# Narrow attention: three of a pair's 52 exponentials computed on VectorE, their probabilities applied later

## The chip, the cores and the metric

One core of a Trainium2 chip runs the whole program. The metric is the device time of one execution in microseconds (us); the time before is the median of three runs. The profile comes from one further execution, recorded by the hardware profiler. Engines are named as in the profile: PE (TensorE matmuls), PEld (TensorE weight loads), DVE (VectorE), ACT (ScalarE), POOL (GpSimd), SP (SyncE).

## The reference, cut to what matters

The reference is a stack of gated cross-attention and feed-forward layers over 2048 tokens of width 256. The change touches one of them, the second cross-attention layer (its tiles are called `c_...` in the profile):

```
q = layernorm(x) @ Wq + bq     # 2048 queries, 16 heads of 16 columns
k = ctx @ Wk + bk              # 1601 keys
v = ctx @ Wv + bv
o = softmax(q k^T / 4) v       # per head
x = x + gate * (o @ Wo + bo)
```

Per head that is 2048 x 1601 exponentials. They are taken without a maximum first as long as a bound on the scores is small, and the sum is divided out at the end: a column of ones in the values gives the sum with the same matmuls.

## The kernel before, in words

The heads go in eight pairs. The keys of one head are 13 tiles (`CT`): twelve of 128 keys and one of 65. A pair therefore has 26 tiles (`TILES`), numbered 0 to 25, head 0 of the pair first. The 2048 queries are split in two halves of 1024, `hp` 0 and 1, so one pair has 52 steps, n = 2t + hp. Each step passes through three stages:

- **Score n** (TensorE, L1888): two matmuls, one on each half of the array's rows, write 128 keys x 1024 queries of scores to two PSUM banks. There are three such double banks, used in turn (`STEP_BANKS`), so score n may be written only when step n-3 has been read.
- **Exponential n** (ScalarE, L1969): one ACTIVATE of 128 x 1024 from PSUM to a buffer `probs` in SBUF. There are four such buffers, `2 * (t % 2) + hp` (they lie in the tiles `c_cT` and `c_wqkv`, whose names the profile shows). The exponential of tile t waits until tile t-2 has been applied, since that tile used the same buffer.
- **Apply t** (TensorE, L1908): four matmuls, one for each 512 queries, each on its own 32 columns of the array, in fp32 and so recorded as two passes each (eight records). They add the tile's values times its probabilities to bank 4 (head 0) or 5 (head 1). Apply t waits for exponential 2t+1.

TensorE runs them in one written order. For each tile t it is: score 2t+3, score 2t+4, apply t. The last two tiles of a pair are t = 24: score 51, score 0 of the next pair, apply 24; and t = 25: score 1 of the next pair, apply 25, then score 2 of the next pair. When a head is complete, VectorE copies the sums (L1987), TensorE turns them with four transposes (L1918: after tile 1 of the next pair for head 1, after tile 14 for head 0), and VectorE divides (L1990, L1994). VectorE also copies each head's values with their ones into `Vh` (L1981). That is all VectorE does here. SyncE loads the next pair's keys and queries when `applied` says that the old ones are free. TensorE's and ScalarE's programs are written out for all pairs; VectorE's pairs 1 to 7 are a loop at run time, so its waits count from a register. A second branch, with maxima, exists for scores above a bound.

Semaphores count the stages: `scored`, `exped`, `applied`, `copied`, `turned`, `normed`, `values_in`.

Of the kernel before, what the change touches and what calls it, by code (L numbers as in the profile page):

```python
# [17 lines left out]
int32 = mybir.dt.int32  # L18
ALU = mybir.AluOpType
# [3 lines left out]
P = 128  # L23
# [3 lines left out]
CT = -(-CTX // P)  # L27
# [3 lines left out]
BANK = 512  # L31
# [1388 lines left out]
CH_HEADS, CH_D = 16, 16  # L1420
GROUP = 4


LH, LD = 8, 64
INNER = LH * LD
# [101 lines left out]
def narrow_attention(nc, m, ci, rows_d, wo_d, bo_d, q_parts, k_parts, pw):  # L1527
# [5 lines left out]
    with ExitStack() as own:  # L1533
# [4 lines left out]
        with ExitStack() as inner:  # L1538
            si = lambda n, s, d=fp32: inner.enter_context(nc.sbuf_tensor(f"c_{n}", s, d))
# [282 lines left out]
            Vh = [si(f"Vh{i}", [P, CT, 32]) for i in range(2)]  # L1822
# [7 lines left out]

            STEP_BANKS = [(0, 2, 6)[n % 3] for n in range(2 * TILES - 1)] + [2]

            EXPED_FOR = {0: -3, 1: 0, 2: -1, 2 * TILES - 1: 2 * TILES - 2}
# [8 lines left out]
            with nc.Block() as block:  # L1842
                @block.sync
                def _(sp):

                    pw.load(sp, qkv_raw, 0)
                    for h in range(2, CH_HEADS):
                        sp.wait_ge(applied, (h - 1) * CT)
                        load_k(sp, h)
                        load_q(sp, h)  # L1850

# [5 lines left out]
                def _(pe):  # L1857
# [19 lines left out]
                    def score(i, n, first=False):  # L1877

                            t, hp = n // 2, n % 2
                            e, r, c0 = t // CT, krows(t), t % CT * P  # L1880
                            if t % CT == 0 and hp == 0:
                                pe.wait_ge(ops_in[e], (i + 1) * OPERANDS)
                            if n >= 3 or not first:
                                pe.wait_ge(exped, i * (2 * TILES) + EXPED_FOR.get(n, n - 2))
                            for b in range(2):
                                q0 = (2 * hp + b) * BANK
                                rows = slice(64 * b, 64 * b + 64)
                                last = nc.tensor.matmul(m.PS[0:r, STEP_BANKS[n] + b, :], Kop[e][rows, c0:c0 + r],  # L1888
                                                        Qop[e][rows, q0:q0 + BANK], start=True, stop=True)
                            last.then_inc(scored, 1)  # L1890

                    def take_maxima(i):

                        pe.wait_ge(row_cleared, i + 1)
                        pe.wait_ge(exped, i * (2 * TILES))
                        for e in range(2):
                            pe.wait_ge(ops_in[e], (i + 1) * OPERANDS)
                            maxima(e, (i * 2 + e) * MAX_REDUCED)
                        pe.wait_ge(max_reduced, (i + 1) * (2 * MAX_REDUCED))

                    def pair(i, first=False, last_pair=False, guarded=False):
                        def apply(t):
# [3 lines left out]
                            pe.wait_ge(exped, i * (2 * TILES) + (2 * t + 2))  # L1906
                            for q in range(4):
                                last = nc.tensor.matmul(m.PS[32 * q:32 * q + 32, 4 + e, :], Vh[e][0:r, t % CT, :],  # L1908
                                                        probs[2 * (t % 2) + q // 2][0:r, (q % 2) * BANK:(q % 2 + 1) * BANK],
                                                        start=(t % CT == 0), stop=(t % CT == CT - 1),  # L1910
                                                        tile_position=(0, 32 * q))
                            last.then_inc(applied, 1)

                        def turn(e, n):

                            pe.wait_ge(copied, n + 1)
                            for j in range(4):
                                last = nc.tensor.transpose(m.PS[:, 4 + e, j * P:(j + 1) * P], outT[e][:, j * P:(j + 1) * P],  # L1918
                                                           m.ident[:])
                            last.then_inc(turned, 1)  # L1920

                        for t in range(TILES):
                            for n in range(2 * t + 3, min(2 * t + 5, 2 * TILES)):
                                score(i, n)

                            if not last_pair and not guarded and t >= TILES - 2:
                                score(i + 1, t - (TILES - 2))
                            apply(t)
                            if t == TURN_AT and not first:
                                turn(1, i * 2 - 1)  # L1930
                            if t == CT + 1:
                                turn(0, i * 2)
                        if not last_pair and not guarded:
                            score(i + 1, 2)
                        if not last_pair and guarded:
# [23 lines left out]
                @block.scalar  # L1959
                def _(act):  # L1960
                    nc.scalar.preload_act_table(ACT.Exp)
                    for i in range(CH_HEADS // 2):
                        for n in range(2 * TILES):
                            t, hp = n // 2, n % 2
                            act.wait_ge(scored, i * (2 * TILES) + (n + 1))
                            if i * TILES + t > 1:
                                act.wait_ge(applied, i * TILES + t - 1)
                            r = krows(t)
                            nc.scalar.activation(probs[2 * (t % 2) + hp][0:r, :],  # L1969
                                                 m.PS[0:r, STEP_BANKS[n]:STEP_BANKS[n] + 2, :].rearrange(  # L1970
                                                     "p b c -> p (b c)"), ACT.Exp).then_inc(exped, 1)

                @block.vector
                def _(dve):
                    bits = dve.value_load(bound[0:1, 0:1].bitcast(int32))

                    def pair(i, first=False):
# [6 lines left out]
                        def output(e, n):  # L1984

                            dve.wait_ge(applied, n * CT + CT)
                            nc.vector.tensor_copy(outT[e][:], m.PS[:, 4 + e, :]).then_inc(copied, 1)  # L1987
                            dve.wait_ge(turned, n + 1)
                            out = m.PS[:, 4 + e, :].rearrange("p (j q d) -> p j q d", q=4, d=32)
                            nc.vector.reciprocal(inverse[e][:], out[:, :, :, CH_D]).then_inc(inverted, 1)  # L1990
                            dve.wait_ge(inverted, n + 1)

                            dst = attended[:, :, ds(n * CH_D, CH_D)].rearrange("p (q j) d -> p j q d", q=4)
                            nc.vector.tensor_tensor(dst, out[:, :, :, 0:CH_D],  # L1994
                                                    inverse[e][:].unsqueeze(3).to_broadcast([P, 4, 4, CH_D]),
                                                    ALU.mult).then_inc(normed, 1)

                        with dve.If(bits > SAFE_BITS):
                            dve.wait_ge(rows_in, 128)
                            dve.wait_ge(exped, i * (2 * TILES))  # L2000
                            for e in range(2):
                                for row in MAX_ROWS:
                                    last = nc.vector.memset(Qop[e][row:row + 1, :], 0.0)
                            last.then_inc(row_cleared, 1)
                            for e in range(2):
                                score_maxima_dve(nc, m, dve, spans, partial, negated, MAX_ROWS,
                                                 [Qop[e][row:row + 1, :] for row in MAX_ROWS], max_scored, max_reduced,
                                                 (i * 2 + e) * MAX_SCORED, (i * 2 + e) * MAX_REDUCED)
                        place_values(0)
                        if not first:  # L2010
                            output(1, i * 2 - 1)
# [7 lines left out]
                    output(1, CH_HEADS - 1)  # L2019

        add_projected(nc, m, "c_out", attended, wo, bo[:].rearrange("p t d -> p (t d)"), m.gate[:, 1:2])

# [1042 lines left out]
```

## Time and profile before

| | us |
|---|---|
| Median of three runs (3122.47 to 3125.54) | 3123.19 |
| The profiled execution's own time | 3124.35 |
| Its span | 3122.6 |
| The narrow attention's stretch of it, first score to last apply | 1960 to 2346 |

The profile's first part gives busy time by engine over the whole span; its second part cuts the span into 40 slices of 78 us, and the narrow attention fills slices 26 to 30 and a part of the next. A time in a timeline is counted from the start of the span. In an x8 row of L1908 the eight pass records of one apply are merged, so its duration is that of the whole apply. An ACTIVATE's start is when it enters its engine, which can be before the one ahead of it has ended; the distance from end to end is what one costs when they follow each other.

### The profile page before, as it was taken

Reading aid. Unit: us, or ns where it says so; the run is one execution under the profiler, and the core shown is the slowest. Engines: PE = TensorE matmul, PEld = TensorE weight load, DVE = VectorE, ACT = ScalarE, POOL = GpSimd, SP = SyncE. Lnnn points to the kernel's source line nnn. Section 1 sums busy time; section 2 is a strip of 40 time slices with the busy share of each in tenths; the row PEclk is TensorE's granted clock in tenths of the full one; section 3 lists DMA queues with packets and bytes.
Section 4 is the critical chain, followed back from the end, with each engine's and each line's share of the span. In section 5 each row is a group of like instructions: output and inputs, shape, how many; then the busy total and the mean of one; then the engine's idle time right before and its main releaser. Section 6 shows DMA issues by size and latency. Waiting matters only on the chain. (4 is left out here: it accounts for less than half of the span.)

```text
span 3122.6 us, 71606 instructions
## 1 busy us (share of the span) xinstructions
PE 2913.0 (93%) x29570; PEld 1454.7 (47%) x29570; DVE 2233.9 (72%) x2810; ACT 1944.9 (62%) x2644; POOL 518.9 (17%) x573
## 2 busy tenths in 40 slices
PE   5999999999999999999999899999996997989979
PEld 3444444444444444444444455222224766556755
DVE  6888888888889888888878875100006886768866
ACT  5665655656656656656556524899993775247642
POOL 0000000000001000000000010200002773247710
PEclk8999999999999999999999989999998999999999
DMA  2000000000000000000000011111101000000000
GB/s 81 9 2 7 3 2 7 3 2 9 2 7 4 2 7 3 2 2 3 2 2 2 28 38 63 56 28 36 29 19 53 15 8 25 36 14 18 5 1 28
DMA packets 30102, 51.69 MB, mean 17 GB/s; under 512 B 6136, under 2 KB 22603, under 8 KB 28619
## 3 DMA queue, kind: packets, MB, share of 16 engines
q1 hardware_dynamic: 29770, 46.91, 4.8%
q8 instruction: 253, 4.15, 0.6%
q14 instruction: 79, 0.64, 0.1%
HBM read 41.04 MB, written 5.83 MB: 15 GB/s over the span
## 5 line engine op out<-in xcount | busy, mean ns | idle before, releaser
L771 ACT ACTIVATE a_probs<-PS 128x1024 f32<-128x1024 f32 x928 | 950.0, 1025 | 572.2 <-PE PS L524 561.4
L537 PE MATMUL PS<-a_probs,a_V 64*64 64x512 f32 x7424 | 984.2, 590 | 6.7 <-DVE a_heads_outT L958 5.0
L1018 DVE TENSOR_TENSOR a_prob_sums<-a_prob_sums,a_probs 128x1024 f32<-128x1024 f32 x512 | 628.5, 1228 | 111.6 <-ACT a_probs L771 85.9
L1015 DVE SCALAR_TENSOR_TENSOR a_prob_sums<-a_probs,a_valid,a_prob_sums 128x1024 f32<-128x1024 f32 x384 | 508.6, 1325 | 73.1 <-ACT a_probs L771 59.4
L524 PE MATMUL PS<-a_Q_hi,a_K_hi 64*64 64x512 f16 x3712 | 390.4, 381 | 6.0 <-ACT a_probs L771 4.9
L524 PE MATMUL PS<-a_Q_hi,a_K_lo 64*64 64x512 f16 x3712 | 387.1, 377 | 2.2 <-issue 2.2
L524 PE MATMUL PS<-a_Q_lo,a_K_hi 64*64 64x512 f16 x3712 | 386.9, 377 | 0.0
L537 PEld LDWEIGHTS PS<-a_probs,a_V 64*64 64x64 f32 x7424 | 293.4, 133 | 168.1 <-issue 23.0
L1969 ACT ACTIVATE c_cT<-PS 128x1024 f32<-128x1024 f32 (+1 forms) x312 | 303.3, 1082 | 1.6 <-PE PS L1908 0.8
L67 POOL CAST a_heads_hi<-a_heads_outT 128x512 f16<-128x512 f32 x31 | 49.6, 1601 | 1444.8 <-DVE a_heads_outT L974 1444.8
L524 PEld LDWEIGHTS PS<-a_Q_hi,a_K_hi 64*64 64x64 f16 x3712 | 119.8, 106 | 260.3 <-issue 254.2
L524 PEld LDWEIGHTS PS<-a_Q_hi,a_K_lo 64*64 64x64 f16 x3712 | 120.6, 107 | 226.2 <-issue 222.0
L1987 DVE COPY c_outT<-PS 128x512 f32<-128x512 f32 x16 | 11.1, 692 | 296.4 <-PE PS L1908 296.4
L1908 PE MATMUL PS<-c_cT,c_Vh 128*32 128x512 f32 (+1 forms) x1248 | 221.1, 607 | 0.3 <-ACT c_wqkv L1969 0.3
L2275 ACT ACTIVATE d_probs<-d_scores,d_minus_max 128x256 f32<-128x256 f32 x256 | 127.0, 497 | 120.3 <-DVE d_minus_max L2440 120.3
L1888 PE MATMUL PS<-c_Qop,c_Kop 64*128 64x512 f16 (+1 forms) x832 | 154.6, 388 | 28.6 <-ACT c_cT L1969 6.7
L524 PEld LDWEIGHTS PS<-a_Q_lo,a_K_hi 64*64 64x64 f16 x3712 | 121.0, 107 | 88.7 <-issue 1.2
L1888 PEld LDWEIGHTS PS<-c_Qop,c_Kop 64*128 64x128 f16 (+1 forms) x832 | 38.6, 94 | 243.9 <-ACT c_cT L1969 194.5
L1969 ACT ACTIVATE c_wqkv<-PS 128x1024 f32<-128x1024 f32 (+1 forms) x104 | 112.9, 1085 | 0.0
L1908 PE MATMUL PS<-c_wqkv,c_Vh 128*32 128x512 f32 (+1 forms) x416 | 109.4, 605 | 0.0
L2543 POOL TENSOR_TENSOR d_crossed<-d_unit,d_tables 128x256 f32<-128x256 f32 x128 | 104.0, 842 | 6.1 <-DVE d_unit L2409 6.1
L2201 PE MATMUL PS<-ident,d_probs 128*128 128x128 f32 x512 | 69.0, 293 | 29.7 <-ACT d_kT L2290 29.7
(356 smaller groups left out, 4616.9 us busy)
## 6 DMA issues: line engine op xcount, KB each, us to landing
c_Qop<-q_part SPq DMA_DIRECT2D x96, 64.0 KB, 2.2
c_Kop<-k_part SPq DMA_DIRECT2D x96, 50.0 KB, 2.0
d_raw<-in_l1f_w_dram SPq DMA_DIRECT2D x18, 256.0 KB, 3.2
d_tables<-in_rotary_dram SPq DMA_DIRECT2D x2, 2048.0 KB, 11.4
X<-in_x_dram SPq DMA_DIRECT2D x2, 1024.0 KB, 9.4
out_dram<-X SPq DMA_DIRECT2D x8, 256.0 KB, 2.2
c_cT<-in_ctxT_dram SPq DMA_DIRECT2D x1, 1601.0 KB, 6.4
a_probs<-in_ctx_dram SPq DMA_DIRECT2D x3, 512.0 KB, 4.9
```

The costliest lines, as they stand in the source:

```text
L67: return engine.tensor_copy(hi, x)
L524: last = nc.tensor.matmul(m.PS[64 * g:64 * g + 64, 2 * (n % 2) + h, :], k[rows, half_keys], q[rows, queries], start=(j == 0), stop=(j == l ...
L537: last = nc.tensor.matmul(m.PS[64 * h:64 * h + 64, PVB + g, :], V[e][rows, s, 64 * h:64 * h + 64], probs[n % 4][rows, h * BANK:(h + 1) * B ...
L771: nc.scalar.activation(probs[n % 4][:], m.PS[:, b0:b0 + 2, :].rearrange("p b c -> p (b c)"), ACT.Exp).then_inc(exped, 1)
L1015: nc.vector.scalar_tensor_tensor(out=sums, in0=new, scalar=valid[:, s:s + 1], in1=sums, op0=ALU.mult, op1=ALU.add).then_inc(summed, 1)
L1018: nc.vector.tensor_tensor(sums, sums, new, ALU.add).then_inc(summed, 1)
L1888: last = nc.tensor.matmul(m.PS[0:r, STEP_BANKS[n] + b, :], Kop[e][rows, c0:c0 + r], Qop[e][rows, q0:q0 + BANK], start=True, stop=True)
L1908: last = nc.tensor.matmul(m.PS[32 * q:32 * q + 32, 4 + e, :], Vh[e][0:r, t % CT, :], probs[2 * (t % 2) + q // 2][0:r, (q % 2) * BANK:(q % ...
L1969: nc.scalar.activation(probs[2 * (t % 2) + hp][0:r, :], m.PS[0:r, STEP_BANKS[n]:STEP_BANKS[n] + 2, :].rearrange("p b c -> p (b c)"), ACT.E ...
L2201: last = nc.tensor.transpose(m.PS[:, SCORE_BANK + 2 * g + p // 2, at:at + P], probs[:, 4 * g + p, kt * P:(kt + 1) * P], m.ident[:])
L2275: last = nc.scalar.activation(probs[:, p, :], scores[:, p, :], ACT.Exp, bias=minus_max[:, p:p + 1], accum_out=sums[:, p:p + 1])
L2543: last = nc.gpsimd.tensor_tensor(crossed[:, qk, :, a, :], unit[w % 2][:, qk, :, 1 - a, :], tables[:, 1, w, qk, a * 32:a * 32 + 32].unsquee ...
```

## The change

Three of a pair's 52 steps are taken by VectorE: both halves of tile 5 (steps 10 and 11) and the first half of tile 20 (step 40). ScalarE skips them. VectorE reads the scores from PSUM, scaled to powers of two and held above -126, in one instruction per step, which frees the bank (`taken`). It then rounds them with a large constant, subtracts, builds the power of two as an integer, and multiplies by a polynomial of degree five: eight further SBUF instructions (after the one or two that take the scores) and one that ends the batch. Steps 10 and 11 are one batch of 2048 columns, step 40 a batch of 1024. The result goes to a buffer of its own, `dve_probs`.

The applies of these steps move. Apply 5 comes behind apply 15. At tile 20 only the half that ScalarE made is applied; the other half is applied behind apply 25, ahead of score 2 of the next pair. The turn of head 0 moves from tile 14 to tile 17. `applied` now counts 27 events per pair in place of 26, and the waits on it and on `exped` are rewritten to match. The wait of an exponential on the reader of its buffer stays the reader two tiles back, save where that was a VectorE step: then it is four tiles back. The banks and their order are unchanged. On VectorE the order within a pair is: values of head 0, output of the last pair's head 1, values of head 1, batch of steps 10 and 11, output of head 0, batch of step 40.

```diff
+            BANK_FROM = {0: 2 * TILES - 4, 1: 2 * TILES - 1, 2: 2 * TILES - 2, 2 * TILES - 1: 2 * TILES - 3}
+            DVE_TILE, DVE_HALF = 5, (CT + 7, 0)
+            DVE_STEPS = (2 * DVE_TILE, 2 * DVE_TILE + 1, 2 * DVE_HALF[0] + DVE_HALF[1])
+            TILE_AT, HALF_AT, TURN_FIRST_AT = CT + 2, TILES - 1, CT + 4
...
-                                pe.wait_ge(exped, i * (2 * TILES) + EXPED_FOR.get(n, n - 2))
+                                owner = BANK_FROM.get(n, n - 3)
+                                back = 1 if n < 3 else 0
+                                if owner in DVE_STEPS:
+                                    pe.wait_ge(taken, i * N_DVE + (DVE_STEPS.index(owner) + 1 - back * N_DVE))
+                                else:
+                                    pe.wait_ge(exped, i * N_ACT + (acted_to(owner) + 1 - back * N_ACT))
...
-                            apply(t)
+                            if t != DVE_TILE:
+                                apply(t, tuple(hp for hp in range(2) if (t, hp) != DVE_HALF))
+                            if t == TILE_AT:
+                                apply(DVE_TILE, (0, 1))
+                            if t == HALF_AT:
+                                apply(DVE_HALF[0], (DVE_HALF[1],))
                             if t == TURN_AT and not first:
                                 turn(1, i * 2 - 1)
-                            if t == CT + 1:
+                            if t == TURN_FIRST_AT:
                                 turn(0, i * 2)
...
                         for n in range(2 * TILES):
+                            if n in DVE_STEPS:
+                                continue
                             t, hp = n // 2, n % 2
                             act.wait_ge(scored, i * (2 * TILES) + (n + 1))
-                            if i * TILES + t > 1:
-                                act.wait_ge(applied, i * TILES + t - 1)
+                            reader = t - 2
+                            if 2 * reader + hp in DVE_STEPS:
+                                reader -= 2
+                            if i * TILES + reader >= 0:
+                                back = 1 if reader < 0 else 0
+                                act.wait_ge(applied, (i - back) * N_EVENTS + event_of(reader + back * TILES, hp))
...
+                        def exponentials(steps, at):
+                            w = len(steps) * 2 * BANK
+                            x, whole, out = exp_in[:, 0:w], exp_whole[:, 0:w], dve_probs[:, 0:w]
+                            count = i * (2 * EXP_STEPS) + at * EXP_STEPS
+                            for k, n in enumerate(steps):
+                                dve.wait_ge(scored, i * (2 * TILES) + (n + 1))
+                                nc.vector.tensor_scalar(exp_in[:, k * 2 * BANK:(k + 1) * 2 * BANK],
+                                                        m.PS[:, STEP_BANKS[n]:STEP_BANKS[n] + 2, :].rearrange("p b c -> p (b c)"),
+                                                        EXP_LOG2E, EXP_LEAST, ALU.mult, ALU.max).then_inc(taken, 1)
+                            dve.wait_ge(taken, i * N_DVE + (DVE_STEPS.index(steps[-1]) + 1))
+                            nc.vector.tensor_scalar(whole, x, EXP_MAGIC, -EXP_MAGIC, ALU.add, ALU.add).then_inc(exp_step, 1)
+                            dve.wait_ge(exp_step, count + 1)
+                            nc.vector.tensor_tensor(x, x, whole, ALU.subtract).then_inc(exp_step, 1)
+                            dve.wait_ge(exp_step, count + 2)
+                            nc.vector.tensor_scalar(whole.bitcast(int32), whole, 127.0, float(2 ** 23), ALU.add,
+                                                    ALU.mult).then_inc(exp_step, 1)
+                            nc.vector.tensor_scalar(out, x, EXP_TERMS[5], None, ALU.mult).then_inc(exp_step, 1)
+                            for j, k in enumerate((4, 3, 2, 1)):
+                                dve.wait_ge(exp_step, count + (4 + j))
+                                nc.vector.scalar_tensor_tensor(out=out, in0=out, scalar=EXP_TERMS[k], in1=x, op0=ALU.add,
+                                                               op1=ALU.mult).then_inc(exp_step, 1)
+                            dve.wait_ge(exp_step, count + EXP_STEPS)
+                            nc.vector.scalar_tensor_tensor(out=out, in0=out, scalar=EXP_TERMS[0], in1=whole, op0=ALU.add,
+                                                           op1=ALU.mult).then_inc(dve_exped, 1)
...
-                        output(0, i * 2)
+                        exponentials(DVE_STEPS[0:2], 0)
+                        output(0, i * 2, i * N_EVENTS + HEAD_END[0])
+                        exponentials(DVE_STEPS[2:3], 1)
```

## Rows read from the trace of the kernel before

**Rows 1.** The page: span and busy time by engine; granted clock in 40 slices.
```profile
span 3122.6 us, 71606 instructions
PE 2913.0 (93%) x29570; PEld 1454.7 (47%) x29570; DVE 2233.9 (72%) x2810; ACT 1944.9 (62%) x2644; POOL 518.9 (17%) x573
PEclk8999999999999999999999989999998999999999
```

**Rows 2.** Stretches of narrow attention: from:to length, busy of each engine, granted clock, DMA.
```profile
2104.00:2152.00 48.00, 44.77 (x324) 9.74 (x320) 3.92 (x8) 47.90 (x53) 0.00 (x0) 1.00 0.12 30
1960.00:2346.00 386.00, 358.48 (x2556) 77.59 (x2556) 29.89 (x61) 383.33 (x417) 18.86 (x18) 1.00 0.11 31
```

**Rows 3.** Timeline of ACT: start us, us, engine, line, operation, tiles.
```profile
2041.87 1.02 ACT L1969 ACTIVATE c_wqkv<-PS 128x1024 f32<-128x1024 f32 x1
...
2052.72 1.17 ACT L1969 ACTIVATE c_wqkv<-PS 128x1024 f32<-128x1024 f32 x1
```

**Rows 4.** Who waited for whom, 2008 to 2344: engine, line, us, times, longest.
```profile
DVE c_outT L1987 <- PE PS L1908: 251.9, 14, 18.2
PEld PS L1888 <- ACT c_cT L1969: 169.7, 238, 1.3
```

**Rows 5.** Timelines of ACT, then PE, one tile amid a head.
```profile
2121.04 2.03 ACT L1969 ACTIVATE c_cT<-PS 128x1024 f32<-128x1024 f32 x2
2122.85 1.14 ACT L1969 ACTIVATE c_wqkv<-PS 128x1024 f32<-128x1024 f32 x1
...
2122.21 0.39 PE L1888 MATMUL PS<-c_Qop,c_Kop 64*128 64x512 f16 x2
2122.53 1.06 PE L1908 MATMUL PS<-c_cT,c_Vh 128*32 128x512 f32 x8
2123.53 0.91 PE L1888 MATMUL PS<-c_Qop,c_Kop 64*128 64x512 f16 x4
```

**Rows 6.** Timeline of PE where one pair passes into the next.
```profile
2104.24 1.06 PE L1908 MATMUL PS<-c_cT,c_Vh 128*32 128x512 f32 x8
2105.42 0.39 PE L1888 MATMUL PS<-c_Qop,c_Kop 64*128 64x512 f16 x2
2105.74 0.62 PE L1908 MATMUL PS<-c_cT,c_Vh 65*32 65x512 f32 x2
...
2106.21 0.60 PE L1908 MATMUL PS<-c_wqkv,c_Vh 65*32 65x512 f32 x2
2106.74 1.07 PE L1888 MATMUL PS<-c_Qop,c_Kop 64*128 64x512 f16 x6
2107.74 1.06 PE L1908 MATMUL PS<-c_cT,c_Vh 128*32 128x512 f32 x8
```

**Rows 7.** Timeline of ACT at the same place; its exponentials 0 and 1.
```profile
2105.43 1.94 ACT L1969 ACTIVATE c_cT<-PS 128x1024 f32<-128x1024 f32 x2
```

**Rows 8.** Groups of DVE by form: busy us, mean ns of one | idle before.
```profile
L2432 DVE TENSOR_TENSOR d_scores<-PS,d_masks 128x1024 f32<-128x1024 f32 x64 | 77.7, 1213 | 3.4 <-PE PS L2133 2.5 <-PE PS L2138 0.9
L1011 DVE TENSOR_SCALAR a_prob_sums<-a_probs,a_valid 128x1024 f32<-128x1024 f32 x32 | 24.1, 753 | 39.4 <-ACT a_probs L771 39.4
L1018 DVE TENSOR_TENSOR a_prob_sums<-a_prob_sums,a_probs 128x1024 f32<-128x1024 f32 x512 | 628.5, 1228 | 111.6 <-ACT a_probs L771 85.9 <-DVE a_prob_sums L1018 0.9 <-DVE a_prob_sums L1015 0.5
L1015 DVE SCALAR_TENSOR_TENSOR a_prob_sums<-a_probs,a_valid,a_prob_sums 128x1024 f32<-128x1024 f32 x384 | 508.6, 1325 | 73.1 <-ACT a_probs L771 59.4
L67 DVE CAST b_W_hi<-b_W1T 128x2048 f16<-128x2048 f32 x1 | 1.2, 1226 | 0.0
```

**Rows 9.** Timeline of DVE in a chain of dependent instructions on small tiles.
```profile
2986.91 0.15 DVE L2709 SCALAR_TENSOR_TENSOR d_work<-d_work 128x4 f32<-128x4 f32 x1
2987.11 0.16 DVE L2711 TENSOR_TENSOR d_work<-d_work 128x4 f32<-128x4 f32 x1
```

**Rows 10.** Timeline of PE: the turn of head 1, and the scores behind it.
```profile
2110.57 0.66 PE L1918 MATMUL PS<-ident,c_outT 128*128 128x128 f32 x4
2111.16 0.60 PE L1888 MATMUL PS<-c_Qop,c_Kop 64*128 64x512 f16 x4
```

More of the change, by code:

```diff
@@ L1421 @@
 GROUP = 4
+EXP_LOG2E, EXP_MAGIC, EXP_LEAST = float(np.log2(np.e)), 12582912.0, -126.0
+EXP_TERMS = (1.00000007, 0.69314697, 0.2402212, 0.05550713, 0.00967554, 0.00132765)
 LH, LD = 8, 64
@@ L1831, in narrow_attention @@
             STEP_BANKS = [(0, 2, 6)[n % 3] for n in range(2 * TILES - 1)] + [2]
-            EXPED_FOR = {0: -3, 1: 0, 2: -1, 2 * TILES - 1: 2 * TILES - 2}
+            BANK_FROM = {0: 2 * TILES - 4, 1: 2 * TILES - 1, 2: 2 * TILES - 2, 2 * TILES - 1: 2 * TILES - 3}
+            DVE_TILE, DVE_HALF = 5, (CT + 7, 0)
+            DVE_STEPS = (2 * DVE_TILE, 2 * DVE_TILE + 1, 2 * DVE_HALF[0] + DVE_HALF[1])
+            TILE_AT, HALF_AT, TURN_FIRST_AT = CT + 2, TILES - 1, CT + 4
+            N_DVE, N_ACT = len(DVE_STEPS), 2 * TILES - len(DVE_STEPS)
+            acted_to = lambda n: n - sum(d < n for d in DVE_STEPS)
+            EVENTS = []
+            for t in range(TILES):
+                if t != DVE_TILE:
+                    EVENTS.append((t, tuple(hp for hp in range(2) if (t, hp) != DVE_HALF)))
+                if t == TILE_AT:
+                    EVENTS.append((DVE_TILE, (0, 1)))
+                if t == HALF_AT:
+                    EVENTS.append((DVE_HALF[0], (DVE_HALF[1],)))
+            N_EVENTS = len(EVENTS)
+            event_of = lambda t, hp: next(i + 1 for i, (u, hps) in enumerate(EVENTS) if u == t and hp in hps)
+            HEAD_END = [max(event_of(t, hp) for t in range(e * CT, (e + 1) * CT) for hp in range(2)) for e in range(2)]
+            exp_in, exp_whole, dve_probs = (si(f"exp_{n}", [P, 4 * BANK]) for n in ("in", "whole", "probs"))
+            EXP_STEPS = 8
+            taken, dve_exped, exp_step = (m.sem(f"c_{n}") for n in ("taken", "dve_exped", "exp_step"))
             partial, negated = si("partial", [P, 1, 2, ST]), si("negated", [P, ST])
@@ L1847, in _ @@
                     for h in range(2, CH_HEADS):
-                        sp.wait_ge(applied, (h - 1) * CT)
+                        sp.wait_ge(applied, (h // 2 - 1) * N_EVENTS + (event_of(CT - 1, 0) if h % 2 == 0 else N_EVENTS))
                         load_k(sp, h)
@@ L1894, in take_maxima @@
                         pe.wait_ge(row_cleared, i + 1)
-                        pe.wait_ge(exped, i * (2 * TILES))
+                        pe.wait_ge(exped, i * N_ACT)
                         for e in range(2):
@@ L1901, in pair, with apply @@
                     def pair(i, first=False, last_pair=False, guarded=False):
-                        def apply(t):
+                        def apply(t, hps):
                             e, r = t // CT, krows(t)
@@ L1905, in apply @@
                                 pe.wait_ge(values_in, i * 2 + (e + 1))
[L1906 to L1910, printed above, removed]
+                            for hp in hps:
+                                if 2 * t + hp in DVE_STEPS:
+                                    pe.wait_ge(dve_exped, i * 2 + (1 if t == DVE_TILE else 2))
+                                else:
+                                    pe.wait_ge(exped, i * N_ACT + (acted_to(2 * t + hp) + 1))
+                            for q in range(2 * hps[0], 2 * hps[-1] + 2):
+                                if 2 * t + q // 2 in DVE_STEPS:
+                                    at = q if t == DVE_TILE else q % 2
+                                    p = dve_probs[0:r, at * BANK:(at + 1) * BANK]
+                                else:
+                                    p = probs[2 * (t % 2) + q // 2][0:r, (q % 2) * BANK:(q % 2 + 1) * BANK]
+                                last = nc.tensor.matmul(m.PS[32 * q:32 * q + 32, 4 + e, :], Vh[e][0:r, t % CT, :], p,
+                                                        start=(t % CT == 0),
+                                                        stop=(event_of(t, q // 2) == max(
+                                                            event_of(u, q // 2) for u in range(e * CT, (e + 1) * CT))),
                                                         tile_position=(0, 32 * q))
@@ L1927, in pair @@
                                 score(i + 1, t - (TILES - 2))
-                            apply(t)
+                            if t != DVE_TILE:
+                                apply(t, tuple(hp for hp in range(2) if (t, hp) != DVE_HALF))
+                            if t == TILE_AT:
+                                apply(DVE_TILE, (0, 1))
+                            if t == HALF_AT:
+                                apply(DVE_HALF[0], (DVE_HALF[1],))
                             if t == TURN_AT and not first:
                                 turn(1, i * 2 - 1)
-                            if t == CT + 1:
+                            if t == TURN_FIRST_AT:
                                 turn(0, i * 2)
@@ L1982, in place_values @@
                                                   ).then_inc(values_in, 1)
-                        def output(e, n):
-                            dve.wait_ge(applied, n * CT + CT)
+                        def exponentials(steps, at):
[22 more added lines that the diff above has]
+                                                           op1=ALU.mult).then_inc(dve_exped, 1)
@@ L1987, in output @@
+                        def output(e, n, end):
+                            dve.wait_ge(applied, end)
                             nc.vector.tensor_copy(outT[e][:], m.PS[:, 4 + e, :]).then_inc(copied, 1)
@@ L1999, in pair @@
                             dve.wait_ge(rows_in, 128)
-                            dve.wait_ge(exped, i * (2 * TILES))
+                            dve.wait_ge(exped, i * N_ACT)
                             for e in range(2):
@@ L2010, in pair @@
                         if not first:
-                            output(1, i * 2 - 1)
+                            output(1, i * 2 - 1, i * N_EVENTS)
                         place_values(1)
-                        output(0, i * 2)
+                        exponentials(DVE_STEPS[0:2], 0)
+                        output(0, i * 2, i * N_EVENTS + HEAD_END[0])
+                        exponentials(DVE_STEPS[2:3], 1)
                         return output
@@ L2018, in _ @@
                         output = pair(j + 1)
-                    output(1, CH_HEADS - 1)
+                    output(1, CH_HEADS - 1, CH_HEADS // 2 * N_EVENTS)
         add_projected(nc, m, "c_out", attended, wo, bo[:].rearrange("p t d -> p (t d)"), m.gate[:, 1:2])
```

## The prediction

> **What bounds the kernel now.** First the page: TensorE is busy 93% of the span and its clock is granted in full nearly everywhere [rows 1]. That average says nothing of this stage, so the second view is the stretches: in 48.00 us amid the narrow attention ScalarE is busy 47.90, TensorE 44.77, VectorE 3.92, at clock 1.00 [rows 2]. The reader should distrust the 44.77: it counts latency. The third view is ScalarE's timeline. Its exponentials end at 2042.89 and 2053.89, twelve apart, so one costs 0.917 us, end to end [rows 3]; 52 of them make 47.7 us (the two of 65 rows a little less), and a pair takes about 48. ScalarE is the bound, and the waits agree: score loads wait 169.7 us for ScalarE, VectorE's output 251.9 us for TensorE [rows 4], while ScalarE waits for nobody.
>
> But by how much is it the bound? That decides this change, and the timeline of one tile tells it [rows 5]. Write E, S, A for exponential, score and apply. An E ends at 2123.07, so the one before it at 2122.16, and S(2t+4) starts at 2122.21: 0.05. The apply starts 0.32 behind it (2122.53), lasts 1.06, and the next score starts at 2123.53, 1.00 after the apply did. A tile thus costs TensorE 1.00 + 0.32 + one more score. Two scores back to back last 0.60 [rows 10] against 0.39 for one [rows 5], so one slot is 0.21 to 0.23; TensorE needs 1.55 of the tile's 1.83 us. It has 0.28 to spare in a tile, and no more.
>
> There is a closed loop beside it. E(2t+4) writes the buffer that A t reads, and A t waits for E(2t+1). From the end of E(2t+1): 0.05 to the score, 0.32 to the apply, 1.06 for it, 0.13 to the start of E(2t+4) (an apply ends at 2105.30, the exponential starts at 2105.43 [rows 6, 7]), and 1.02 for it, as the unhurried ones last [rows 3, 7]: 2.59 us (the rounded terms make 2.58). Three exponentials take 2.75. **So the loop of four probability buffers stands only 0.16 us behind ScalarE.**
>
> **Part by part.** I set the end of the last pair's E51 to zero and follow one pair.
>
> *Removed:* three exponentials a pair, 3 x 0.917 = 2.75 us, in eight pairs 22.0 us of ScalarE. What of it comes back is what the loops let through.
>
> *Steps 10 and 11.* E12 is in tile 6 and waits for A4; A4 waits for E9. With 10 and 11 gone, E12 is the very next one, and it still ends 2.59 after E9. Before, it ended 2.75 after. Two exponentials removed return 0.16 us. ScalarE sits idle about 1.5 us in their place. The banks aren't late: E12 needs S12, E13 needs S13, which waits behind A4 anyway and for `taken`, done by then (below). Sum -0.16.
>
> *Apply 5 behind apply 15, and the turn at tile 17.* Let U be the end of E31. A15 starts U+0.37, A5 0.91 later (two passes of 0.455: in an apply the passes start at 2105.74 and 2106.2 [rows 6]), S35 at U+2.28, done +2.67, so E35 starts U+2.80 and ends +3.82, against 4 x 0.917 = 3.67. A16 then starts U+2.83, is done +3.89, and E36 ends U+5.04. A17 and the turn (0.59, from 2110.57 to 2111.16 [rows 10]) keep TensorE busy: S41 starts only at U+7.50, so E41 ends at U+9.04; S42 U+7.84, A19 U+8.16, done +9.22, E42 ends U+10.37. Before, E42 ended eleven exponentials behind E31, 10.08, plus 0.13 that the turn cost it (a delay of the same kind follows each turn). So this stretch, with step 40 taken out of it, comes to +0.16 us. The third removed exponential too returns nothing.
>
> *The second half of tile 20 behind apply 25.* This is new work: a half apply takes two of the array's four column groups for as long as a whole one, since the four matmuls of a pass run side by side (eight records of 0.60 in 1.06 us [rows 6]). Before, A25 started at 2105.74 and score 2 of the next pair at 2106.74 [rows 6]. It was done at 2107.13, and E2 followed E1 (end 2107.37 [rows 7]) without loss, ending 2108.28. Now score 2 starts at 2107.65, E2 starts at 2107.65 + 0.39 + 0.13 = 2108.17 and ends 2109.19: +0.90. In the last pair there is no next one, but the output waits 0.91 for it. TensorE could absorb it elsewhere (0.28 a tile); here two exponentials only are in store behind it.
>
> Per pair -0.16 + 0.16 + 0.90 = +0.90. It falls on seven passages, and the end adds 0.91: 7 x 0.90 + 0.91 = 7.2 us.
>
> *Terms that no row shows.* An apply behind an apply costs 0.91, if it follows as a pass follows a pass, or 1.00, as a score follows an apply. With 1.00 both late applies cost more, the pair +1.06: 8.5 in all. I lean to 0.91, the same form of instruction. Each apply now has two waits in place of one. Nothing in the trace shows a second wait on TensorE; it is 0 where it hides in the 0.32 between score and apply, and I bound it at 0.03 an apply, which in the tight places (about eight per pair) makes up to 1.6 us in all. Below: if a half apply costs half, 0.46, the passages cost 0.45 and the whole 3.6. I take 7.8 and keep 3.6 to 10.
>
> *VectorE, the cover of all this.* Reading 1024 scores from PSUM: 1.21 (L2432, the nearest row with PSUM) [rows 8]. In SBUF a one-input instruction of 1024 costs 0.75, of 2048 1.23 to 1.29 (the cast of 2048; 0.75 + 512 elements at the two-a-cycle slope), a two-input one 1.23 and 2.30, a scalar-tensor-tensor 1.33 and 2.40 [rows 8]; a dependent one follows after 0.05 (2987.06 to 2987.11) [rows 9]. First batch: 2 x 1.21 + 3 x 1.29 + 2.30 + 5 x 2.40 + 10 x 0.04 = 21.0. Second: 1.21 + 3 x 0.75 + 1.23 + 5 x 1.33 + 0.4 = 11.7. With the 3.92 of before, 36.6 of 48.8 us. What matters is lateness. E7 ends at 8.40 (1.09 for E0, seven pitches, and the 0.90 above), S10 follows at 8.45 and is done at 8.85, so the first batch ends at 30.0; A5 wants it at 31.5: 1.5 to spare. S40 is done at 36.8; VectorE has by then given out head 0 (its turn ends at 36.3), takes it at 37.2 and ends at 48.9; the half apply wants it at 50.05: 1.2 to spare. Values for the next pair (0.59) are wanted at 51.8. Step 11's bank is free at 11.5, score 14 wants it at 12.0; step 40's at 38.4, S43 wants it at 39.4. So VectorE costs nothing, with 1.2 us of margin. The bound above: all three one-input instructions at one element a cycle (2.30 and 1.23, as the two-input rows). That adds 3.0 to the first batch, 1.5 over its margin, and with it about 1.6 us per pair: +13.
>
> A page of the Trainium skill prices ScalarE itself. "VectorE: DVE Perf Modes", in its section on the TRN2 errata, gives PSUM to SBUF as 172 cycles plus one per element at 1.2 GHz, that is 0.997 us for 1024, an estimate by that page; the rows have 0.917 from end to end and 1.02 alone. By the page's price 24 exponentials would be 23.9 us rather than 22.0, and the loop would look slower than ScalarE by less; the rows decide. The same page's tier table gives fp32 `tensor_scalar` in SBUF two elements a cycle and anything from PSUM one, which rows 8 bear out for forms without a bitcast.
>
> **Sum.** 3124.35 + 7.8 = 3132.2 for a profiled run. The median before lies 1.16 below that run's own time, so 3131.0.
>
> **The rivals.**
> *It pays: ScalarE's time comes back.* If E12 and E42 really start behind E9 and E41, every pair gives back 2.75, pays 0.90 at its end and 0.3 at apply 5: -1.5 x 8, near 3111; half of it back gives 3120. For it: ScalarE busy 47.90 of 48.00. Against it: E0 starting 0.13 behind an apply's end [rows 6, 7], with its 1.02 alone, shows that the buffer wait is real, and each number of the loop is read off. It decides if the loop is under 1.8 us rather than 2.59. Chance 0.09.
> *Too small to tell* (0.2% is 6.2 us, about what a measurement of this kernel can tell from no change): the half apply at half its price, or one of the stalls milder than drawn: 3125 to 3129. Against the half price: the passes of four matmuls end together. The page "TensorE: Matmul & The Clock Gate", part 3 on packing, has tiles side by side for about 4 ns each, which is the same side; the sum doesn't use it. Chance 0.23, and in it is that the change does nothing at all.
> *VectorE is late.* 2.30 instead of 1.29, or 0.2 us between dependent steps: 3132 to 3145, with 3144 where all go at one element a cycle. For it: its waits count from registers in a loop, and no row has a bitcast. Against: margins of 1.2 and 1.5. Chance 0.18.
> *My forecast*, the ring closes and the half apply is paid: 3130 to 3134, chance 0.50.
>
> **How the numbers follow.** The likeliest case gives 3131.0. The range takes in the bounds of the small terms below (3126) and most of a late VectorE above (3145). Faster by over 0.2%: 0.09. Within: 0.23. Slower: 0.68.
>
> **What would show it.** ScalarE's timeline: a gap of about 1.5 us between E9 and E12 in every pair, released by L1908 and not by scores; a gap of 0.9 at E2 behind the passage, released by a score; end to end still 0.917 elsewhere; ScalarE busy near 45 of 48. Pairs 48.8 apart rather than 47.9. VectorE busy near 37 a pair, one-input instructions of 2048 near 1.3 us, and TensorE not waiting for its last instruction (the end of a batch). If pairs are 46 to 47 apart, the loop was wrong; if TensorE waits for VectorE before apply 5 or at the pair's end, the third rival is it.

## The result, and the profile after

The changed kernel takes 3129.9 us (median of 14 runs, 3126.71 to 3132.07) against 3123.53 for the kernel before in the same runs (14, 3118.55 to 3127.59). The ratio is 1.0021, with a 95% interval of 1.0013 to 1.0029: slower, by 6.4 us between the medians, and by more than noise. I had forecast 3131.0, which is 7.8 us above the median of the three runs before. The profiled execution took 3130.8 us, its span 3129.0.

The page of the changed kernel, against [rows 1]: ScalarE lost 19 us of busy time, VectorE gained 243, and the span is 6.4 us longer.

```profile
span 3129.0 us, 72043 instructions
PE 2915.5 (93%) x29570; PEld 1457.0 (47%) x29570; DVE 2477.1 (79%) x2978; ACT 1925.7 (62%) x2620; POOL 532.6 (17%) x573
```

In the changed kernel's own lines the exponentials are L2019, the scores L1917, the applies L1946. A stretch of 48 us amid the narrow attention, against [rows 2] (length, busy of PE, PEld, DVE, ACT, POOL, clock, DMA):

```profile
2110.00:2158.00 48.00, 44.06 (x318) 9.66 (x312) 33.72 (x29) 44.88 (x50) 0.00 (x0) 1.00 0.12 30
```

ScalarE now idles 3.1 of 48 us, so the relief arrived at the engine. It was not used. Who waited for whom between 2012 and 2348, against [rows 4], where ScalarE had no row:

```profile
ACT c_cT L2019 <- PE PS L1946: 15.9, 21, 1.6
...
ACT c_cT L2019 <- PE PS L1917: 4.8, 7, 0.7
PEld PS L1917 <- DVE c_exp_in L2041: 5.9, 7, 0.8
```

ScalarE waits for applies (L1946) 21 times, three times in each of the seven pairs of the window, and once a pair for a score (L1917). The waits for VectorE are only for the reads of its scores; no row has TensorE waiting for the end of a batch. The ScalarE timeline shows where, with the end of the last pair's E51 at 2106.67 (against [rows 7] and [rows 3]):

```profile
2105.61 1.06 ACT L2019 ACTIVATE c_wqkv<-PS 65x1024 f32<-65x1024 f32 x1
2106.70 1.94 ACT L2019 ACTIVATE c_cT<-PS 128x1024 f32<-128x1024 f32 x2
2109.32 1.02 ACT L2019 ACTIVATE c_cT<-PS 128x1024 f32<-128x1024 f32 x1 [0.69 <-PE PS L1917]
...
2114.95 1.94 ACT L2019 ACTIVATE c_cT<-PS 128x1024 f32<-128x1024 f32 x2
2118.46 2.85 ACT L2019 ACTIVATE c_cT<-PS 128x1024 f32<-128x1024 f32 x3 [1.57 <-PE PS L1946]
...
2140.79 2.86 ACT L2019 ACTIVATE c_cT<-PS 128x1024 f32<-128x1024 f32 x3 [0.27 <-PE PS L1946]
...
2146.13 1.02 ACT L2019 ACTIVATE c_cT<-PS 128x1024 f32<-128x1024 f32 x1 [0.42 <-PE PS L1946]
```

E2 waits 0.69 us for its score; E12 waits 1.57 for apply 4; E36 waits 0.27 and E42 waits 0.42 for applies. From the end of E9 (2114.95 + 1.94 = 2116.89) to that of E12 (start 2118.46, 1.02 long, 2119.48) are 2.59 us.

TensorE at the same two places: first the passage with the half apply, whose four records read `c_exp_probs`, against [rows 6]; then score 12, which follows the end of E9, and apply 4, against [rows 5].

```profile
2106.73 0.39 PE L1917 MATMUL PS<-c_Qop,c_Kop 64*128 64x512 f16 x2 [0.16 <-ACT c_wqkv L2019]
2107.05 0.62 PE L1946 MATMUL PS<-c_cT,c_Vh 65*32 65x512 f32 x2
...
2107.93 1.03 PE L1946 MATMUL PS<-c_exp_probs,c_Vh 128*32 128x512 f32 x4
2108.89 0.82 PE L1917 MATMUL PS<-c_Qop,c_Kop 64*128 64x512 f16 x6
...
2116.94 0.39 PE L1917 MATMUL PS<-c_Qop,c_Kop 64*128 64x512 f16 x2 [0.25 <-ACT c_cT L2019]
2117.26 1.07 PE L1946 MATMUL PS<-c_cT,c_Vh 128*32 128x512 f32 x8
```

VectorE's two batches in the same pair, against [rows 8]:

```profile
2115.42 2.54 DVE L2041 TENSOR_SCALAR c_exp_in<-PS 128x1024 f32<-128x1024 f32 x2 [0.52 <-PE PS L1917]
2117.99 1.23 DVE L2045 TENSOR_SCALAR c_exp_whole<-c_exp_in 128x2048 f32<-128x2048 f32 x1
2119.26 2.29 DVE L2047 TENSOR_TENSOR c_exp_in<-c_exp_in,c_exp_whole 128x2048 f32<-128x2048 f32 x1
2121.58 1.23 DVE L2049 TENSOR_SCALAR c_exp_whole<-c_exp_whole 128x2048 int32<-128x2048 f32 x1
...
2133.28 2.29 DVE L2057 SCALAR_TENSOR_TENSOR c_exp_probs<-c_exp_probs,c_exp_whole 128x2048 f32<-128x2048 f32 x1
...
2153.17 1.23 DVE L2057 SCALAR_TENSOR_TENSOR c_exp_probs<-c_exp_probs,c_exp_whole 128x1024 f32<-128x1024 f32 x1
```

The first batch runs from 2115.42 to 2135.57, the second ends at 2154.40. Apply 5 starts at 2138.09 and the half apply at 2156.6, which is 49.9 us after the end of the last pair's E51: 2.5 and 2.2 us of room for VectorE. The integer step with its bitcast (L2049) takes 1.23 us, as its one-input neighbour L2045 does.

Below, a pair's length is the distance from the end of the last pair's E51 to the end of its own (the first pair's is taken from the start of its E0). It was 47.91 us in every pair but the first, and is 48.66 to 48.67 now.

### The profile page after: what moved, and what is told of

The parts are those of the page before. It is cut to its first block and busy times, and to the rows that moved or that the text cites. A ratio compares the mean times of both kernels' runs of the same rounds, so it can differ in the third digit from the quotient of the medians.

```text
span 3129.0 us, 72043 instructions
## 1 busy us (share of the span) xinstructions
PE 2915.5 (93%) x29570; PEld 1457.0 (47%) x29570; DVE 2477.1 (79%) x2978; ACT 1925.7 (62%) x2620; POOL 532.6 (17%) x573
## 5 line engine op out<-in xcount | busy, mean ns | idle before, releaser
L771 ACT ACTIVATE a_probs<-PS 128x1024 f32<-128x1024 f32 x928 | 949.2, 1024 | 571.6 <-PE PS L524 567.0
L2019 ACT ACTIVATE c_cT<-PS 128x1024 f32<-128x1024 f32 (+1 forms) x296 | 286.5, 1055 | 25.1 <-PE PS L1946 19.0
L1946 PE MATMUL PS<-c_cT,c_Vh 128*32 128x512 f32 (+1 forms) x1184 | 212.6, 608 | 0.5 <-ACT c_wqkv L2019 0.5
L1917 PE MATMUL PS<-c_Qop,c_Kop 64*128 64x512 f16 (+1 forms) x832 | 149.1, 387 | 34.1 <-ACT c_cT L2019 16.3
L1917 PEld LDWEIGHTS PS<-c_Qop,c_Kop 64*128 64x128 f16 (+1 forms) x832 | 36.6, 94 | 235.8 <-ACT c_cT L2019 169.7
L2054 DVE SCALAR_TENSOR_TENSOR c_exp_probs<-c_exp_probs,c_exp_in 128x2048 f32<-128x2048 f32 (+1 forms) x64 | 113.7, 1776 | 2.2
L2019 ACT ACTIVATE c_wqkv<-PS 128x1024 f32<-128x1024 f32 x96 | 101.6, 1058 | 0.0
L1946 PE MATMUL PS<-c_wqkv,c_Vh 128*32 128x512 f32 (+1 forms) x384 | 101.0, 605 | 0.0
```

The costliest lines, as they stand in the source:

```text
L771: nc.scalar.activation(probs[n % 4][:], m.PS[:, b0:b0 + 2, :].rearrange("p b c -> p (b c)"), ACT.Exp).then_inc(exped, 1)
L2019: nc.scalar.activation(probs[2 * (t % 2) + hp][0:r, :], m.PS[0:r, STEP_BANKS[n]:STEP_BANKS[n] + 2, :].rearrange("p b c -> p (b c)"), ACT.E ...
L2054: nc.vector.scalar_tensor_tensor(out=out, in0=out, scalar=EXP_TERMS[k], in1=x, op0=ALU.add, op1=ALU.mult).then_inc(exp_step, 1)
```

## The experiments

All are compared with the kernel before, on the same chip.

**Tile 5 alone on VectorE** (`e1_tile_only`).

```diff
-            DVE_TILE, DVE_HALF = 5, (CT + 7, 0)
-            DVE_STEPS = (2 * DVE_TILE, 2 * DVE_TILE + 1, 2 * DVE_HALF[0] + DVE_HALF[1])
+            DVE_TILE, DVE_HALF = 5, None
+            DVE_STEPS = (2 * DVE_TILE, 2 * DVE_TILE + 1)
...
-                        exponentials(DVE_STEPS[2:3], 1)
```

> Only steps 10 and 11 go to VectorE (apply 5 behind apply 15, turn at tile 17); step 40 stays on ScalarE, so nothing is applied behind apply 25. Theory (the loop of four probability buffers): E12 still ends 2.59 us after E9, two exponentials removed return 0.16, and the late apply with the later turn takes 0.2 to 0.3 back: a pair lasts 48.0 us (47.9 before), the whole +0.9 us over before (0 to +2). E2 follows E1 without a gap. Rival, ScalarE's time comes back: pairs of 46.1 to 46.5, -11 to -15 us. Rival, VectorE's presence itself costs (PSUM port, memory): +5 us as the full change has.

Measured 3124.17 against 3122.53, ratio 1.0004 (0.9995 to 1.0013); pairs of 48.03 us. Two exponentials are gone and ScalarE still waits 1.57 us behind E9:

```profile
2114.27 1.94 ACT L2019 ACTIVATE c_cT<-PS 128x1024 f32<-128x1024 f32 x2
2117.77 2.86 ACT L2019 ACTIVATE c_cT<-PS 128x1024 f32<-128x1024 f32 x3 [1.57 <-PE PS L1946]
```

This part of the change, with two thirds of its relief, gives nothing back and costs 0.12 us a pair: E12 comes 0.16 earlier, and the late apply 5 with the later turn takes 0.28 again. VectorE's work isn't what costs either: its batch is 20 us a pair here.

**The half of tile 20 alone** (`e2_half_only`).

```diff
-            DVE_TILE, DVE_HALF = 5, (CT + 7, 0)
-            DVE_STEPS = (2 * DVE_TILE, 2 * DVE_TILE + 1, 2 * DVE_HALF[0] + DVE_HALF[1])
+            DVE_TILE, DVE_HALF = None, (CT + 7, 0)
+            DVE_STEPS = (2 * DVE_HALF[0] + DVE_HALF[1],)
...
-                        exponentials(DVE_STEPS[0:2], 0)
```

> Only step 40 goes to VectorE, its half applied behind apply 25. Theory: the cost of the change is this half apply. E2 of the next pair is 0.76 late as in the full change, step 40 returns 0.16 to 0.2 and the turn at tile 17 a little: pairs of 48.35 (47.9 before), the whole +3.9 us over before (+3 to +5). Rival, the cost lies in apply 5 and batch one: 0 to +1 us. Rival, ScalarE's time comes back: pairs of 47.0, -7 us.

Measured 3126.3, ratio 1.0012 (1.0003 to 1.0022), +3.8 us by the medians; pairs of 48.42. E2 ends 3.67 us after the last E51, as with the full change (3.68), against 2.92 before.

**The full change without the half apply** (`e5_no_half_apply`).

```diff
-                if t == HALF_AT:
-                    EVENTS.append((DVE_HALF[0], (DVE_HALF[1],)))
...
-                            if t == HALF_AT:
-                                apply(DVE_HALF[0], (DVE_HALF[1],))
```

> The full change, but the half apply behind apply 25 is left out (VectorE still makes its probabilities, and they are used by nobody: the output lacks one half tile's share). Theory: of the change's 0.75 us a pair all is this apply, by way of score 2; without it E2 follows E1, and pairs last 47.8 (47.9 before, 48.66 with the change), the whole -1 to +1 us against before. Rival: the cost is VectorE's work or ScalarE's idle time: pairs stay near 48.5, +5 us.

Measured 3123.26 against 3122.62, ratio 1.0003 (0.9994 to 1.0012); pairs of 47.87, where the change has 48.66. Together with e2 this settles where the cost lies: the 0.75 us a pair that the change costs is the half apply at the passage. (This kernel leaves one half tile's share out of the output.) What is left of the change, all three exponentials removed, is worth 0.04 us a pair.

**Six buffers in the kernel before** (`e3_before_6bufs`).

```diff
+            SLOTS = 3
+            probs += [si(f"more_probs{i}", [P, 2 * BANK]) for i in range(2 * SLOTS - 4)]
...
-                            if i * TILES + t > 1:
-                                act.wait_ge(applied, i * TILES + t - 1)
+                            reader = next(u for u in range(t - 1, t - 1 - TILES, -1) if u % TILES % SLOTS == t % SLOTS)
+                            if i * TILES + reader >= 0:
+                                act.wait_ge(applied, i * TILES + reader + 1)
```

> The kernel before with six probability buffers in place of four (two more of 128 x 1024, reader three tiles back inside a pair; at the passage it is two back as before), nothing on VectorE. Theory: with no exponential removed the loop was 0.16 us behind ScalarE and costs only the two bumps of 0.13 a pair: pairs of 47.6, -2 us (-3 to -1). Rival: the buffers bound nothing, 0. Rival: the ring held ScalarE back at each tile: over -5 us.

Measured 3121.1 against 3122.53, ratio 0.999 (0.9981 to 0.9999); pairs of 47.41, where I had 47.6. ScalarE is busy 48.00 of 48.00 us:

```profile
2104.00:2152.00 48.00, 45.09 (x328) 9.74 (x320) 3.92 (x8) 48.00 (x53) 0.00 (x0) 1.00 0.12 30
```

The ring of four buffers cost 0.50 us a pair before the change. By the ends of the exponentials in both traces, 0.27 of it stood behind the two turns (0.13 and 0.14) and 0.09 at the passage, where E0 now ends 1.00 us after E51 rather than 1.09; the rest is spread in small steps over the pair. I had counted the two turns only.

**Six buffers in the changed kernel** (`e6_after_6bufs`). The edit is e3's on the changed kernel; the reader also skips VectorE's steps.

> The full change with six probability buffers (reader three tiles back), order of TensorE untouched. Theory: E12 now waits for score 12 only and ends 1.5 us after E9 rather than 2.59, E13 for score 13 behind apply 4; the half apply still costs 0.8 at each passage. Pairs of 47.3, which is -5 us, of which the first pair loses 1 to 3 us, since VectorE's first batch runs there beside GpSimd and ends late: -2 to -5 us against before, that is -8 to -11 against the change. Rival, the buffers don't matter: pairs of 48.6, +6 us.

Measured 3120.05 against 3122.62, ratio 0.9991 (0.9982 to 1.0000), at the edge of what can be told from no change; the pairs of 47.27 in the trace are clear. That is 1.39 us a pair less than the change with four buffers, from the same work on each engine. E12 now waits for its score, 0.49 us, instead of 1.57 for an apply:

```profile
2108.34 1.10 ACT L2020 ACTIVATE c_wqkv<-PS 128x1024 f32<-128x1024 f32 x1
2109.93 1.02 ACT L2020 ACTIVATE c_cT<-PS 128x1024 f32<-128x1024 f32 x1 [0.49 <-PE PS L1919]
2111.25 1.94 ACT L2020 ACTIVATE c_cT<-PS 128x1024 f32<-128x1024 f32 x2 [0.29 <-PE PS L1919]
```

Between 2012 and 2330 ScalarE no longer waits for any apply, so the four buffers were what held it at these places. But they held back only a part of the three exponentials. Of the 1.39 us, 0.50 is what the two buffers give with nothing removed (e3); 0.89 is what they let through of the 2.75 removed. Against e3, with six buffers on both sides, E2 comes 0.85 later and the pair is still 0.14 shorter, so about 1.0 of the 2.75 us comes back, where with four buffers it was 0.04. What holds the rest is the scores: E12, E13 and E41 wait 0.49, 0.29 and 0.50 us for theirs.

**Tile 5 alone, six buffers, score 13 ahead of apply 4** (`e4_tile_6bufs_look`): e1 and e3 together, and in TensorE's order (score 13 is written ahead of apply 4)

```diff
-                            for n in range(2 * t + 3, min(2 * t + 5, 2 * TILES)):
+                            ahead = lambda u: 2 * u + 5 + (u == DVE_TILE - 1)
+                            for n in range(ahead(t - 1) if t else 3, min(ahead(t), 2 * TILES)):
```

> Steps 10 and 11 on VectorE as in the change, none of tile 20, six probability buffers, and score 13 written ahead of apply 4. Theory: E12 then waits only for its score, which waits for E9's bank: it ends 0.05+0.39+0.05+1.02 = 1.5 us after E9, so about 1.2 of the removed 1.83 us comes back, with no half apply behind the pair: pairs of 46.4, -11.8 us against before (-9 to -13). Rival, the buffers were not the limit and the scores' banks or TensorE are: 47.6 or more, -2 us or worse. Rival, late apply 5 costs as much as the tile gives: -2 us.

Measured 3114.12 against 3122.53, ratio 0.9971 (0.9960 to 0.9982), with pairs of 46.38 us (46.4 expected). That is 1.65 less than e1, which removes the same two exponentials, and 1.03 less than e3, which removes none. What the order of the score is worth was not run alone; E13 ends 2.83 us after E9 in e6 and 2.43 here, so by an estimate from these about 0.4 us of a pair is its share. But the first pair took 49.99. Its VectorE and GpSimd timelines:

```profile
1973.09 2.57 DVE L2049 TENSOR_TENSOR c_exp_in<-c_exp_in,c_exp_whole 128x2048 f32<-128x2048 f32 x1
...
1978.80 10.42 DVE L2056 SCALAR_TENSOR_TENSOR c_exp_probs<-c_exp_probs,c_exp_in 128x2048 f32<-128x2048 f32 x4
1989.25 3.13 DVE L2059 SCALAR_TENSOR_TENSOR c_exp_probs<-c_exp_probs,c_exp_whole 128x2048 f32<-128x2048 f32 x1
...
1974.35 12.72 POOL L67 CAST qkv_hi<-c_qkv_raw 128x512 f16<-128x512 f32 x6
```

The four chained instructions take 10.42 us beside GpSimd and the last one 3.13 (by then GpSimd has gone on from its casts to two-input instructions, L71), where they take 9.27 and 2.29 in the other pairs; GpSimd's six casts take 12.72 us instead of 3.4. The whole batch takes 23.2 us for 20.2, and apply 5 waits for it.

**The same, with GpSimd's split held back** (`e8_pool_held`): `pool.wait_ge(dve_exped, 1)` ahead of it.

> The kernel with steps 10 and 11 on VectorE, six buffers and score 13 ahead (run before at 0.9971), with GpSimd's splitting of the next layer's weights held until VectorE's first batch is done. Theory: in the first pair VectorE's instructions ran 12% longer beside GpSimd (2.58 for 2.29) and one took 3.1, so the batch ended 3 us late and the first pair lasted 49.99 for 46.8; held back, the first pair takes 46.8 and the whole -11 to -12 us against before. The split then meets the second pair's batch only if it lasts over 25 us. Rival: VectorE's length in the first pair has another cause (start, clock): first pair stays at 50, -8.5 us. Rival: the split is wanted sooner, and its lateness shows behind the attention: -8 or less.

Measured 3110.78 us (5 runs, 3108.65 to 3114.55) against 3122.62, ratio 0.9964 (0.9950 to 0.9977): the lowest median of all, 11.8 us under the kernel before and about 19 under the change, though its interval overlaps that of e4. The first pair lasts 46.61, the others 46.40. Both engines run at their own pace:

```profile
1976.44 9.27 DVE L2057 SCALAR_TENSOR_TENSOR c_exp_probs<-c_exp_probs,c_exp_in 128x2048 f32<-128x2048 f32 x4
1985.74 2.29 DVE L2060 SCALAR_TENSOR_TENSOR c_exp_probs<-c_exp_probs,c_exp_whole 128x2048 f32<-128x2048 f32 x1
...
1996.84 3.41 POOL L67 CAST qkv_hi<-c_qkv_raw 128x512 f16<-128x512 f32 x6
```

VectorE's batch is back to 20.2 us. The first pair is 3.4 us shorter than in e4, but holding GpSimd back is not all of that. TensorE's granted clock falls from 1.00 to 0.50, the lower of its two levels, near the attention's start in every trace; in this one TensorE had idled 1.48 us just before its first score, as in e4. It stays there 3.5 us (1960.7 to 1964.2 here), but in e4 6.9 (1960.4 to 1967.3). E7 ends 8.88 us after the pair's start in e4 and 7.70 here: 1.2 of the 3.4 us are there before VectorE has read a score. The other 2.2 come between E34 and E35, where e4 waits for the batch. So the expectation's rival of another cause had a part in it. What set the length of the slow stretch was not tried.

**More work for VectorE** (`e7_more_dve`), to measure its room.

```diff
+            more = si("exp_more", [P, 2 * BANK])[:]
...
+                            for spare in (more, exp_in[:, 2 * BANK:], exp_whole[:, 2 * BANK:]) if len(steps) == 1 else ():
+                                nc.vector.tensor_tensor(spare, x, x, ALU.mult)
```

> The full change with three more VectorE instructions of 128 x 1024 (1.23 us each, 3.7 in all) in the batch of step 40, to measure how much room VectorE has. Theory: the batch ended at 47.7 of 48.66 and the half apply wanted it at 49.9, 2.2 us of room; 3.7 more make it 1.5 us late at first, and the lateness goes round with VectorE's other work: pairs of 50.2 to 50.4, +20 us against before. Rival, VectorE had no room and was already the bound: pairs of 52.3. Rival, it has 3.7 us of room: 48.7.

One run, 3136.27 us, 13.7 over the kernel before, where I expected 20; pairs of 49.82, that is 1.15 more than the change, where I expected 1.5 to 1.7. Now TensorE does wait for the batch, at each of the six passages whose half apply lies in the window, by the row of its loads:

```profile
ACT c_cT L2020 <- PE PS L1918: 13.0, 7, 1.9
PEld PS L1947 <- DVE c_exp_probs L2060: 11.2, 6, 1.9
```

The three instructions overlap their neighbours by 0.08 to 0.09 each and add 3.4 us, not 3.7. 3.4 less 1.15 is 2.2 us of room, which is what the changed kernel's timeline shows. My expectation had let the lateness grow round the loop; it does not.

## Why the prediction was right, step by step

The forecast was slower by 7.8 us; the medians of the same runs say 6.4 (3129.9 less 3123.53). By terms, per pair:

| step | forecast us | measured us |
|---|---|---|
| passage: half apply ahead of score 2 | +0.90 | +0.76 |
| steps 10 and 11: E9 to E12 | 2.59 for 2.75: -0.16 | 2.59: -0.16 |
| apply 5, turn at 17, step 40: up to E42 | +0.16 | +0.12 |
| tile 20 to the pair's end | 0 | +0.03 |
| sum of a pair | +0.90 | +0.75 |
| the end of the last pair | +0.91 | +0.91 |

The forecast's 7.8 has 7.2 from these terms; measured they make about 6.2, and the other 0.6 is the allowance below.

*ScalarE is the bound but the loop is right behind it.* Right. E12 ended 2.59 us after E9 by the very numbers read from the trace before, and e6 shows the other side: with the loop opened a part of the time comes back, 0.89 us a pair beyond what the buffers give by themselves. The rival "it pays" was wrong for this kernel. e8 gets to pairs of 46.4, but it isn't the same change: it removes two exponentials and not three, has no half apply, six buffers, one score moved ahead and GpSimd held back. The plain comparison is e1 with e4, the same two exponentials removed: 48.03 and 46.38, by two buffers and the order of one score.

*The half apply.* The mechanism and its place were right: e2 has it alone, e5 is without it. Its size was off by 0.14, in two terms. I took 0.13 us from a score's end to the exponential, read off a place where the exponential waited for an apply. A score's end is followed after 0.04: the score starts at 2108.89, lasts 0.39, and E2 starts at 2109.32. And the half apply pushed score 2 by less than 0.91. An apply behind an apply costs 0.88 (2107.05 to 2107.93), the half one 0.96 before the next score (2107.93 to 2108.89): 1.84 for both, where one apply ahead of a score cost 1.00. So the half apply costs 0.84, and not half of that: with two of the four column groups it lasts 1.03 us, with four 1.07.

*The allowance for a second wait per apply*, 0.6 of the 7.8, was not needed. Apply 4 starts 0.32 behind its score, as before.

*VectorE hides.* Right, and with more room than I gave it (2.5 and 2.2 us for 1.5 and 1.2): I had priced a scalar-tensor-tensor of 2048 at 2.40 from a mean of 1.33 for 1024; undisturbed it is 2.29. The rule that I named from the Trainium skill ("VectorE: DVE Perf Modes", the section with the tier table) holds for the bitcast too: 1.23 us for 2048 from SBUF, two elements a cycle, and 1.21 to 1.22 for 1024 from PSUM, one a cycle. Before, the only row from PSUM, L2432, had two inputs and so showed nothing for a one-input form; L2041 now does.

*A slip that entered no sum.* By the price of 0.997 us that the prediction takes from the Trainium skill ("VectorE: DVE Perf Modes", TRN2 errata) three exponentials are 2.99 us and the loop 2.57, so the loop would stand about 0.4 us behind ScalarE, further than the 0.16 and not nearer. The 0.16 was measured.

*What I missed* is the first pair. VectorE's batch there ran beside GpSimd and took 22.3 us for 20.2; it ended 31.25 us after the pair's start, and apply 5 started at 31.50. In the changed kernel that used up nearly all the room without costing (the first pair took 48.75 and was 48.79), in e4 it cost about 2.2 us. The Trainium skill's page "SBUF — State Buffer", in its section "Who interferes with whom", has VectorE and GpSimd share a port pair under an exclusive lock, held for a whole instruction. On GpSimd's side the rows agree: a cast of 0.62 us lasted 2.67 beside instructions of 2.58. VectorE's instruction grew by 0.29 (2.58 for 2.29), less than one cast, so the rows don't show that it waits for whole casts.

## What to carry to other kernels

Before taking work off the bound engine, find the loop that stands next behind it, and by how much: here a ring of four buffers, 2.59 us for three exponentials of 2.75. Work taken out at one spot gives back no more than that distance, since its neighbours in the ring stay where they are; ring depth and the order of issue have to change with it. And where a late piece of work is put matters more than its size: a whole late apply amid the pair cost 0.28 us (e1, with the moved turn), half an apply ahead of score 2 cost 0.75 (e2). That the half apply would have been cheap elsewhere follows from this but was not tried.

## What the runs showed of the hardware

A 128x1024 exponential from PSUM costs ScalarE 0.917 us behind another and 1.02 alone. An exponential starts 0.04 us after the score it waits for, 0.13 after the apply that frees its buffer; why they differ was not tried. Fp32 passes on two of the array's four column groups take as long as on four (1.03 us for the two passes of a half apply, 1.06 to 1.07 for those of a whole one). Beside GpSimd casting in SBUF, VectorE's two-input instructions of 2048 took 2.57 to 2.59 us for 2.29, beside GpSimd's own two-input instructions (L71) one took 3.13, and GpSimd's casts took up to four times their own length (2.67 for 0.62); GpSimd held back, both were undisturbed. TensorE's granted clock stood at 0.50 for 3.4 to 3.5 us near the attention's start, in one trace (e4) for 6.9, and at 1.00 from 1968 on.
